# Quantised weights kept as bf16 instead of int8, and their DMAs issued from SyncE instead of GpSimd

## The reference

```python
def act_quant(x):                       # per token, 8 bits
    scale = 127.0 / jnp.clip(jnp.max(jnp.abs(x), axis=-1, keepdims=True), 1e-05)
    return jnp.clip(jnp.round(x * scale), -128, 127) / scale

def weight_quant(w):                    # one scale per matrix, values -1, 0, 1
    scale = 1.0 / jnp.clip(jnp.mean(jnp.abs(w)), 1e-05)
    return jnp.clip(jnp.round(w * scale), -1, 1) / scale

x = x + attention(layernorm(x), w_qkv, w_out)     # 16 heads of 64
y = layernorm(x)
h = act_quant(y) @ weight_quant(w1).T             # 1024 -> 4096
h = silu(depthwise_conv1d(h, conv_w, conv_b))     # 3 taps over the tokens
x = x + act_quant(h) @ weight_quant(w2).T         # 4096 -> 1024
```

## Time and profile before

| | |
|---|---|
| median of 10 runs | 19804.84 us (19791.55 to 19813.61) |
| the profiled execution | 19804.49 us, span 19802.9 us |
| spans of the 8 cores | 19758.5 to 19802.9 us |
| busy shares | PE 48%, PE weight load 26%, DVE 24%, ACT 7%, POOL 3% |
| chain that ended last, by engine | PE 36%, DMA 23%, DVE 20%, issue 9%, ACT 6%, SP's queue 4% |
| granted TensorE clock, mean | 0.616 of 2.4 GHz |
| DMA, mean | 26 GB/s; 1,466,609 of 1,502,577 packets under 512 B |

### The profile page before, as it was taken

The page is one execution under the profiler, slowest core; times in us unless marked ns, Lnnn a source line. Parts: engine busy times, 40 slices in busy tenths (PEclk is TensorE's granted clock), DMA queues, the critical chain, the costliest instruction groups (busy, mean ns, idle before and its releaser), DMA issues.

```text
span 19802.9 us, 116457 instructions; the slowest of 8 cores (19758.5 to 19802.9 us)
## 1 busy us (share of the span) xinstructions
PE 9551.3 (48%) x31134; PEld 5136.5 (26%) x31396; DVE 4836.2 (24%) x10661; ACT 1299.2 (7%) x3100; POOL 673.3 (3%) x756
## 2 busy tenths in 40 slices
PE   0013664664565566623333466466466456653333
PEld 0012332332333233111111233233233233211111
DVE  4431111111111211154442111111111111124444
ACT  0000110010010010010000010011011001000000
POOL 0010000000000000001111000000000000001111
PEclk9996556556555555566666655655655655557666
DMA  3331001001000000123333100100100100014333
GB/s 77 91 92 40 0 0 38 6 0 30 14 0 21 22 0 12 39 29 36 36 34 65 30 0 5 38 0 0 42 1 0 34 9 0 24 36 44 34 34 35
DMA packets 1502577, 520.50 MB, mean 26 GB/s; under 512 B 1466609, under 2 KB 1466994, under 8 KB 1499890
## 3 DMA queue, kind: packets, MB, share of 16 engines
q0 software_dynamic: 610816, 176.23, 8.1%
q1 hardware_dynamic: 891122, 336.80, 6.5%
HBM read 386.83 MB, written 58.72 MB: 22 GB/s over the span
## 4 chain that ended last, share of the span: by engine, by line
PE 36%; DMA 23%; DVE 20%; issue 9%; ACT 6%; SPq 4%; DVEq 1%; ACTq 0%; POOLq 0%; POOL 0%
PE pb L734 11%; PE pb L784 11%; PE pb L767 6%; DMA wq_stage<-s_wqkvT_hi 6%; ACT attn_sb L754 5%; DVE attnT_sb L774 4%; DMA wq_stage<-s_wqkvT_lo 4%; DMA wo_stage<-s_woutT_hi 4%; SPq L299 4%; PE pb L1298 2%; DMA w_ring<-s_w2qT 2%; DMA w_ring<-s_w1qT 2%; PE pb L1069 2%; DMA su_w<-w 1%; DVE pb L749 1%
## 5 line engine op out<-in xcount | busy, mean ns | idle before, releaser
L784 PE MATMUL pb<-v_tok,attnT_sb 128*128 128x64 f32 x8704 | 2157.5, 425 | 1201.2 <-DVE attnT_sb L774 1201.2
L784 PEld LDWEIGHTS pb<-v_tok,attnT_sb 128*128 128x128 f32 x8704 | 1954.3, 327 | 1662.7 <-issue 1662.7
L734 PE MATMUL pb<-kqf 64*128 64x512 f32 (+3 forms) x2560 | 2324.5, 1010 | 22.1 <-DVE mbias L694 22.1
L594 PE MATMUL pb<-wq_stage,xst_ring 128*128 128x512 bf16 x2944 | 1405.3, 502 | 1708.2 <-DMA xst_ring<-s_xhat_lo 1708.0
L774 DVE COPY attnT_sb<-pb 128x512 f32<-128x512 f32 (+3 forms) x1280 | 782.9, 612 | 5253.1 <-PE pb L767 5253.1
L767 PE MATMUL pb<-ident_f,attn_sb 128*128 128x128 f32 x4352 | 1228.4, 429 | 1708.2 <-ACT attn_sb L754 1708.2
L767 PEld LDWEIGHTS pb<-ident_f,attn_sb 128*128 128x128 f32 x4352 | 766.9, 215 | 3356.8 <-issue 3356.8
L754 ACT ACTIVATE attn_sb<-pb,mbias 128x512 f32<-128x512 f32 (+3 forms) x1280 | 798.3, 624 | 7554.7 <-PE pb L734 4688.6
L599 PE MATMUL pb<-wq_stage,xst_ring 128*128 128x256 bf16 x3072 | 1053.8, 343 | 164.9 <-DMA xst_ring<-s_xhat_hi 122.1
L594 PEld LDWEIGHTS pb<-wq_stage,xst_ring 128*128 128x128 bf16 x3072 | 380.0, 124 | 2510.0 <-issue 2371.1
L1298 PE MATMUL pb<-hq_t,w_ring 128*128 128x512 bf16 (+1 forms) x2002 | 593.0, 442 | 895.6 <-DVE hq_t L1270 455.1
(11 more groups left out here) (185 smaller groups left out, 6174.7 us busy)
## 6 DMA issues: line engine op xcount, KB each, us to landing
w_ring<-s_w1qT POOLq DMA_DIRECT2D x256, 256.0 KB, 3.2
w_ring<-s_w2qT POOLq DMA_DIRECT2D x256, 256.0 KB, 3.3
wq_stage<-s_wqkvT_hi SPq DMA_DIRECT2D x768, 64.0 KB, 1.9
wq_stage<-s_wqkvT_lo SPq DMA_DIRECT2D x768, 64.0 KB, 1.9
su_w<-w SPq DMA_DIRECT2D x64, 512.0 KB, 3.5
su_w<-w SPq DMA_DIRECT2D x16, 2048.0 KB, 8.2
xst_ring<-s_xhat_hi SPq DMA_DIRECT2D x1024, 32.0 KB, 1.8
xst_ring<-s_xhat_lo SPq DMA_DIRECT2D x1024, 32.0 KB, 1.8
```

The costliest lines, as they stand in the source:

```text
L594: ef=spf, pk=pkq, ws=wsl: e.matmul(pk[:, 0:512], self.xst_ring[:, xs_, :], self.wq_stage[:, ws, wp, 0:512], start=sf, stop=ef, skip_group_ ...
L734: kb=kb, kl=klen, sb=sbank: e.matmul(sb[:, 0:kl], self.kqf[64 * hh:64 * hh + 64, 2 + pair, qc * P:(qc + 1) * P], self.kqf[64 * hh:64 * hh ...
L784: e.matmul(self.PB[6][:, 64 * hh:64 * hh + 64], self.attnT_sb[:, atsl, c * P:(c + 1) * P], self.v_tok[:, kb * 4 + c, 64 * hl:64 * hl + 64] ...
```

## The change

The two DRAM tensors of quantised weights become bf16, so that neither the stores nor the loads cast. The stores of the quantised weights in the setup, the loads of the first product and the loads of the second product go from POOL's queue to SP's. The bytes that a load reads in DRAM double (runs of 256 B in place of 128 B); those that it writes in SBUF are the same. All that is computed stays the same.

```diff
-        self.s_w1qT = nc.dram_tensor("s_w1qT", [ND, NF1, P, P], I8).ap()
-        self.s_w2qT = nc.dram_tensor("s_w2qT", [NF1, ND, P, P], I8).ap()
+        self.s_w1qT = nc.dram_tensor("s_w1qT", [ND, NF1, P, P], BF16).ap()
+        self.s_w2qT = nc.dram_tensor("s_w2qT", [NF1, ND, P, P], BF16).ap()
...
                 ev_busy = self.st(dap.transpose([1, 0, 2]), src,
-                                  wait=tev, q="gpsimd", dsem="dwst0")
+                                  wait=tev, q="sync", dsem="dwst0")
...
                 self.s_w1qT[:, fc].transpose([1, 0, 2]),
-                wait=merge(self.wprep_tok, self.w12_busy[wsl]), q="gpsimd",
+                wait=merge(self.wprep_tok, self.w12_busy[wsl]), q="sync",
                 dsem=f"dw12_{wsl}")
...
                     wait=merge(self.wprep_tok, self.w12_busy[wsl]),
-                    q="gpsimd", dsem=f"dw12_{wsl}")
+                    q="sync", dsem=f"dw12_{wsl}")
```

## The result

The changed kernel takes 19359.05 us (median of 8 runs, 19346.21 to 19380.2) against 19805.19 (median of 29 runs of the kernel before). The ratio is 0.9776, with a 95% interval of 0.9768 to 0.9785: 446 us less, where 334 were forecast. 19,470 us was predicted, with 19,250 to 19,780 as the range.

What follows compares the result with a forecast made beforehand. No engine bounds the kernel; chains of waits do. Terms -402 - 15 - 67 + 109 + 29 + 12 = -334 us take 19804.5 to 19,470 us, range 19,250 to 19,780.

Steps and rivals of the forecast that it cites:

- The block at the accumulating DMA: Second product, windows 1 to 3: next m's loads no longer queue behind the accumulating DMA; six stages, -402 us.
- The walk of an m: Second product: batch-by-batch timing of one m after the change, 10.60 us, raised by 0.4 to 11.0 against 12.1.
- X: Both products: time from a batch's end to use of the next load, falling from 3.95 to 3.30 us.
- The first product: Feed-forward block: X falls 0.65 us over 128 pairs, 83 us; one pair in five gains nothing: -67 us.
- Setup, w1: Preparation of w1: next tile's load waits behind this tile's store on SP; 31 tiles x 3.5 us, +109 us.
- Setup, w2: Preparation of w2: four stores quicker, next load later; 26 us, and 3 for passages between matrices, +29 us.
- L: SP's queue: time from issue to landing of a 256 KB transfer in 256-byte packets, taken as 3.0 us.
- the first (L over 4.3): Rival: SP's queue is slower for many small packets, L passes 4.3; 19,970 us at L = 5.0; chance 0.10.
- the third (near 2.2): Rival: L on SP's queue is near 2.2 us, giving 19,270 us; chance 0.12.
- The second: Rival: two loads in flight delay each other by half a microsecond, L = 3.6 in effect, 19,620 us; chance 0.18.
- The fourth: Rival: busier PE is granted the lower clock in both products' stages; +64 us, or 19,870; chance 0.03.
- The fifth: Rival: accumulating DMA's block goes only in part, `qrow` or semaphores bind; half of 402 us lost, 19,670; chance 0.05.

Runs made afterwards that it cites:

- The third experiment: Kernel before (int8, all on POOL), with the accumulating DMA of an m emitted behind the first two loads of the next m: 19482.16 us, ratio 0.9854.
- the last two profiles: Kernel before, four slots, accumulating DMA behind four loads: 0.9553; changed kernel, setup load ahead of stores, four slots, run once more: 0.9554.
- the first kernel with four slots: Changed kernel with the next su_w load ahead of the stores, plus all four weight slots used in both products: 18935.42 us, ratio 0.9542.
- the first and the fourth experiment: Changed kernel with setup stores back on POOL: 0.9724; changed kernel with the next su_w load ahead of this tile's stores on SP: 0.9717.
- the second and the third: Changed kernel with all three DMAs back on POOL (only bf16 left): 1.0039; kernel before with the accumulating DMA behind two loads: 0.9854.

## Why the prediction was right, and where its sizes were off

1. **The block at the accumulating DMA**: the mechanism was right, -420 against -402, but the size agrees in part by luck. The stage before was read too long: 161 and 165 us in the earlier trace rows go on to the last accumulating DMA, while window 0's 101 ends with its last matmul. From like ends (155.5 and 158.7) the same working gives some 380 us. The stage after was forecast too long as well, 94 and 98 us where it took 84.5 and 92.9. The walk of an m gave 10.6 us, and the trace has 10.4; the prediction said 11.0, because I had added 0.4 us, window 0 of before showing 12.1 where the walk gave 11.7. That came from X, which was 4.26 there (8882.57, the end of a batch, to 8886.83), not 3.95, and went with it. What I did not say is that the order alone would give some 285 of it: the prediction put all of it down to taking the loads out of POOL's queue. The third experiment leaves some 135 for the quicker load, for the accumulating DMA that there still stands ahead of the third batch's load, and for the granted clock (0.84 to 0.90 there, 0.97 on SP).
2. **The first product**: the mis-sized term, -112 against -67. The page of the profile splits it: PE's idle time before L1069 fell from 277.6 to 193.0 us, 85 less, where X (0.65 us by 128 pairs) had given 83; and the matmuls were busy for 531.0 us before and 500.7 after, 30 less (both roughly, since some matmul records are missing before). So the step that failed is the one on the clock. I took one pair in five as gaining nothing, 16 us off, where the clock gave 30 us back: three stages of before, granted 0.82 to 0.88, took 103 to 106 us, and after no stage was under 0.94 from its first matmul to its last. X itself was read from a single row, and the 797 us of the earlier trace rows are 9 short of the eight stages' 805.9. The five stages of before with a granted clock of 0.94 and more take 98.3 us on average, 6.14 per pair, so X was 4.24 and not 3.95; after, a stage takes 86.7 us, 5.42 per pair, X = 3.5 and not 3.3. Both were too low by much the same, so their difference, 0.72, is near the 0.65.
3. **Second product, window 0**: -30 against -15. X fell from 4.26 to 3.25 in the rows, not from 3.95 to 3.30.
4. **Setup, w1**: right, 3.1 us per tile for 3.5 (2.56 for the later issue, the rest for the load: 3.8 us against 3.5 from issue to landing). 31 tiles are 97 us, not 109; the queueing of the load's packets behind the store's costs 0.3 to 0.6 us, not 1.0.
5. **Setup, w2**: +12 against +26. The stores land in 2.5 us, not 3.0, so a copy follows a copy after 3.54 us (0.69 and the wait of 2.85), not 3.9, and the next tile starts 9.0 us after the last copy, not 9.7; a tile takes 1.7 us more, not 3.7. The 5 us that are then left of the 114 lie in the passages between the matrices and the preparation of the other weights; 3 were forecast.
6. **End of a sample**: right, +6.2 and +4.2 against 5.8 each.
7. **L**: 2.9 us, where 3.0 was taken from the growth between the nearest sizes on SP's queue and POOL's 3.2. The Trainium skill's first-byte times (page "DMA: Bandwidth & Descriptors", section "Latency and other measured facts"), 0.4 us apart, gave an estimate of 2.8. The measured 2.9 for loads lies between the two, and the stores' 2.8 and 2.5 are nearer to the page's. But the 3.2 was that of a load with a cast: between like loads, bf16 without a cast, the two queues are 0.6 us apart (3.5 and 2.9), not 0.4, so that the estimate came close partly by chance.

Of the rivals, the first (L over 4.3) and the third (near 2.2) are excluded by the landing of 2.9. The second, two loads in flight delaying each other, had its mark in L = 3.6; the loads of both products overlap, and X = 3.25 in the steady rows (9406.05, the end of a batch, to 9409.30), so it fell too. With four slots, where more loads can be in flight, the landing on SP's queue was 3.0 to 3.4 us in one run and 2.9 to 3.1 in the other; no experiment was made on this alone. The fourth, a lower clock in denser stages, went the other way (0.75 to 0.97) and stayed away in the densest kernels (0.95 to 0.98), apart from single stages: two at 0.79 to 0.82 in each of the last two profiles. The fifth did not occur: the accumulating DMA leaves 4.3 us after an m of 10.4. In the sum the errors had one sign, 18 + 15 + 45 + 24 + 2 us, and with the 8 left over they are the 112 us by which the gain was larger. The first of them is itself the difference of two larger ones.

What stays open is a part of X on POOL. Issue (0.58), landing (3.2) and start (0.17) make 3.95, and the average was 4.24. The trace gives 0.24 for the start in the first product, and a mean landing of 3.2 to 3.4 in those five stages (single loads took up to 4.7), which makes 4.04 to 4.19. Why the granted clock of single stages differs (0.79 to 0.98) between windows of like density was not tried either.

## What to carry to other kernels

A DMA queue is an engine that works in order: before a DMA is moved to a quicker queue, look at what stands in front of it and what will stand behind it, since here one waiting DMA ahead of the loads cost some 285 us by its place alone, and the move made the same mistake anew with the setup's load behind its store (+114 us, gone when the load was put ahead of the store). An operation that waits for the end of a step belongs behind as many prefetches as the ring has slots; behind fewer the rest of the ring is lost (107 to 115 us against 70 a stage). And where the wait is latency, a deeper ring takes it away whole, while a quicker queue only shortens it: two slots more brought the kernel from 0.972 to 0.954, and with them, and the accumulating DMA behind all four loads, the two queues were equal.

## What the runs showed of the hardware

- A load of 256 KB in 1024 packets of 256 B lands 2.9 us after its issue from SP, 3.5 from POOL without a cast, and 3.2 from POOL with a cast from int8, which reads half the bytes in DRAM. I had not expected the cast to be the quicker form. These are the kernels with two slots; with four slots the medians lie between 2.9 and 3.4 from SP and between 3.2 and 3.6 from POOL with a cast.
- The same size written to DRAM lands after 2.5 to 2.8 us from SP (3.2 from POOL), and after 3.2 from SP in one run, for w1 in the first kernel with four slots.
- The 24 loads `su_w<-wqkv` of 512 KB, which the change does not touch, land after 4.3 us in the kernel after and 3.5 in the one before. On one chip they took 3.9 and 4.2 in the first and the fourth experiment and 3.6 in the second and the third, on another 3.7 with four slots on SP, and on a third 4.1 with the same kernel. What sets this was not found; it is worth at most 24 x 0.8 = 19 us.
- The share of time in which the DMA engines are busy is no measure of bytes: in the first product it is 0.80 for int8 from POOL at 81 GB/s, 0.30 for bf16 from POOL at 80 GB/s and 0.42 for bf16 from SP at 96 GB/s. So it is the loads with a cast that show the high share, not those of POOL's queue.
